# Thirteen embedding tables looked up by products instead of twelve, and gathers issued in step with TensorE's lookups

## The chip, the cores and the metric

The kernel runs on one core of a Trainium2 chip. The metric is the time of one execution on the device, in microseconds (us). The kernel before takes 147.07 us (median of 3 runs, 146.13 to 147.31).

## What is computed

A recommendation tower: 26 embedding tables are read at 512 samples, each sample's 27 vectors (the dense one and 26 rows) are multiplied with each other, and the 351 products above the diagonal go with the dense vector through three layers.

```python
e = jnp.stack([tbl_0[ids[:, 0]], ..., tbl_25[ids[:, 25]]], axis=1)        # 512 x 26 x 128, f32
combined = jnp.concatenate([dense[:, None, :], e], axis=1)                # 512 x 27 x 128
inter = jnp.einsum('bnd,bmd->bnm', combined, combined)[:, TRIU_I, TRIU_J] # 512 x 351
h = jnp.concatenate([dense, inter, dense], axis=1)                        # 512 x 607
h = jnp.maximum(h @ W_top1 + b_top1, 0.0)                                 # 512 x 512
h = jnp.maximum(h @ W_top2 + b_top2, 0.0)                                 # 512 x 256
y = h @ W_top3                                                            # 512 x 1
```

Tables have 1000, 1250, 12500 or (table 6) 125000 rows of 128 f32 values.

## The kernel before, in words

The 512 samples are four tiles of 128. A table's rows come to `xt` (128 features on the partitions; sample, table along the free dimension) in one of two ways.

**Lookup by product.** Twelve small tables (`ONEHOT_TABLES`) are loaded whole, with 8 rows to each of 125 partitions (10 rows for the one with 1250 rows; these counts are `CHUNKS`). For a lookup VectorE compares the ids of all 512 samples with the row numbers of each chunk (L552, one 125x512 mask for a chunk; the tables of a unit in `UNITS` are compared by one instruction, so a unit of two has masks of 125x1024). ScalarE makes the mask of the last chunk in two steps (L626, L631). ScalarE rounds the table to a high part (L616), VectorE subtracts that from the table, in two halves, for a low part (L561, `make_low`). TensorE then multiplies high and low part of each chunk with its mask (L363): 16 products for a table of 8 chunks, 20 for one of 10, all into one bank. ScalarE copies the bank to `xt` (L637). Two units of masks, two pairs of parts and four table buffers are in use in turn; a table's load waits until the low part of the table four before it is made. The last lookup is in two pieces, samples 0 to 127 before the first tile's products, the rest after them. A semaphore `lookup_done` counts the pieces.

**Gather.** The other 14 tables are gathered: GpSimd issues one indirect DMA (L332) for each table and tile, 128 rows of 512 bytes, 56 in all, tile by tile. After each one it writes a buffer that nobody reads (`unread`, L340) and waits for the write before that. From tile 2 on, a tile's gathers wait until the rows of the tile two before it have been taken. A tile's 14 tables are four groups (`GROUP_SIZES`); for a group TensorE transposes the rows (L377) and ScalarE copies them to `xt` (L644, one copy for each run of neighbouring tables). `AFTER_LOOKUP`, `IN_GRAM`, `IN_GAP`, `BEFORE_GRAM` and `AFTER_LAYER2` give the place of each of the 16 groups in TensorE's order.

**Products and layers.** For each sample there is one 27x27 product (L398, `gram`), in two halves of 64 samples for each tile; each is two matmuls in the trace, f32 operands being taken in two passes, so a half is 128 matmuls there. VectorE transposes the result into place and copies the triangle (L580, L591), TensorE turns it (L414), and the layers follow (L425, L436, L452). Products of tile t+1 stand between the halves of layer 1 of tile t. All orders are written out by hand; each engine runs its queue in order. W_top1 (1280 KB) is loaded by SyncE after the last table.

Of the kernel before, what the change touches and what calls it, by code (L numbers as in the profile page):

```python
# [29 lines left out]
F32 = mybir.dt.float32  # L30
# [5 lines left out]
P = 128  # L36
# [10 lines left out]

ONEHOT_TABLES = [4, 10, 11, 17, 19, 20, 24, 25, 3, 0, 8, 14]  # L50
VP = 125
CHUNKS = [8] * 9 + [10] + [8] * 2
CH = max(CHUNKS)
SIZES = sorted(set(CHUNKS))
FIRST_COLUMN = {c: sum(x + 1 for x in SIZES if x < c) for c in SIZES}
ROW_COLUMNS = sum(c + 1 for c in SIZES)

UNITS = [[0], [1, 2], [3, 4], [5, 6], [7, 8], [9], [10, 11]]
UNIT_OF = [u for u, members in enumerate(UNITS) for _ in members]
COMPARED = [CHUNKS[members[0]] - 1 for members in UNITS]  # L60
BEFORE_UNIT = [sum(COMPARED[:u]) for u in range(len(UNITS))]
UNIT_RING = 2
IDROW_RING = 3
SLOTS = max(CHUNKS[members[0]] * len(members) for members in UNITS)
assert sum(UNITS, []) == list(range(len(CHUNKS))) and all(len({CHUNKS[h] for h in m}) == 1 for m in UNITS)


LOW_BEFORE = []
_owed = []
for _u, _members in enumerate(UNITS):  # L70
    _end = COMPARED[_u]
# [6 lines left out]
VP_A = VP // 16 * 16  # L78
NOH = len(ONEHOT_TABLES)
TABLE_RING = 4  # L80
# [6 lines left out]

GATHERED = [f for f in range(F) if f not in ONEHOT_TABLES]
SOURCES = [f + 1 for f in GATHERED]
GROUP_SIZES = [4, 4, 3, 3]  # L90
GROUP_STARTS = [sum(GROUP_SIZES[:i]) for i in range(len(GROUP_SIZES))]
GROUPS = [(t, SOURCES[i:i + k]) for t in range(TILES) for i, k in zip(GROUP_STARTS, GROUP_SIZES)]
assert sum(GROUP_SIZES) == len(SOURCES)

AFTER_LOOKUP = [[], [], [], [0], [1], [2], [3], [4], [5], [6], [7], []]
IN_GRAM = [8]
IN_GAP = [9]
BEFORE_GRAM = [[], [], [14, 15]]  # L100
AFTER_LAYER2 = [[10, 11], [12, 13], []]
ORDER = sum(AFTER_LOOKUP, []) + IN_GRAM + IN_GAP
for _t in range(TILES - 1):
    ORDER += BEFORE_GRAM[_t] + AFTER_LAYER2[_t]
assert ORDER == list(range(len(GROUPS)))
GROUPS_UP_TO = [sum(t <= tile for t, _ in GROUPS) for tile in range(TILES)]

WARM_UP = 13
HIGH, LOW = PARTS = range(2)


# [43 lines left out]
def build(nc, dense_by_column, ids, ids_by_table, tables, w1, w2, columns, identity, out):  # L155
    with ExitStack() as ctx:
        def sb(name, shape, dt):
            return ctx.enter_context(nc.sbuf_tensor(name, shape, dt))

        def sem(name):  # L160
            return ctx.enter_context(nc.semaphore(name))
# [61 lines left out]
        lookup_done = sem("lookup_done")  # L223
# [3 lines left out]
        gram_done = sem("gram_done")  # L227
# [5 lines left out]
        h1_done = sem("h1_done")  # L233
# [8 lines left out]
        def unit_onehot(u, c):  # L242

            members = UNITS[u]
            chunks = CHUNKS[members[0]]
            slots = onehot[:, u % UNIT_RING, 0:len(members) * chunks, :]
# [25 lines left out]
        def load_first_table(queue, a, b):  # L272
            n = CHUNKS[0] * D
            rows = tables[ONEHOT_TABLES[0]].rearrange("(p c) d -> p (c d)", c=CHUNKS[0])
            queue.dma_start(table_sb[a:b, 0, 0:n], rows[a:b, :]).then_inc(table_landed[0], 16)

        unread = sb("unread", [P, 256], F32)
        unread_written = sem("unread_written")

        block = ctx.enter_context(nc.Block())  # L280

        @block.sync
        def _(sp):
            def load_table(h):
                s, f = h % TABLE_RING, ONEHOT_TABLES[h]
                u = UNIT_OF[h]
# [29 lines left out]
        @block.gpsimd  # L316
        def _(pool):

            for c in SIZES:
                first = FIRST_COLUMN[c]  # L320
                pool.iota(row_id[:, first:first + c], [[1, c]], base=0, channel_multiplier=c,
                          allow_small_or_imprecise_dtypes=True).then_inc(row_id_ready, 1)
                pool.iota(row_id[:, first + c:first + c + 1], [[1, 1]], base=1 - c, channel_multiplier=-c,
                          allow_small_or_imprecise_dtypes=True).then_inc(row_id_ready, 1)
            pool.wait_ge(ids_landed, 16)
            paced = 0
            for g, (t, features) in enumerate(GROUPS):
                if t >= ROWS_RING and t != GROUPS[g - 1][0]:
                    pool.wait_ge(group_turned, GROUPS_UP_TO[t - ROWS_RING])
                for n in features:  # L330
                    f = n - 1
                    pool.indirect_dma_start(  # L332
                        rows_sb[:, t % ROWS_RING, GATHERED.index(f), :], None, tables[f],
                        bass.IndirectOffsetOnAxis(ids_sb[:, t, f:f + 1], 0),
                    ).then_inc(group_landed[g], 16)

                    if paced:
                        pool.wait_ge(unread_written, paced)
                    paced += 1
                    pool.memset(unread[:, :], 0.0).then_inc(unread_written, 1)  # L340

        @block.tensor
        def _(pe):
# [141 lines left out]
            pe.wait_ge(zeros_ready, 1)  # L485
            for _ in range(WARM_UP):
                pe.matmul(ps_z[:, 0, :], zeros[:, 0:P], zeros[:, :], start=True, stop=True)  # L487


            for h in range(NOH):  # L490
                lookup(h)
                for g in AFTER_LOOKUP[h]:
                    turn_group(g)
            gram(0, 0)
            for g in IN_GRAM:
                turn_group(g)
            gram(0, 1)
            lookup(NOH - 1, 1)
            for g in IN_GAP:
                turn_group(g)  # L500
# [3 lines left out]
            for t in range(TILES - 1):  # L504

                layer1_pairs(t, 0)
                for g in BEFORE_GRAM[t]:
                    turn_group(g)
# [3 lines left out]
                for half in range(2):  # L512
                    layer2(t, half)
                for g in AFTER_LAYER2[t]:
                    turn_group(g)
# [91 lines left out]
        def _(act):  # L607
# [26 lines left out]
            def copy_lookup(h, piece=0):  # L634
                act.wait_ge(lookup_done, h + piece + 1)
                a, b = COLUMNS[h][piece]
                act.copy(xt[:, a // RUN:b // RUN, ONEHOT_TABLES[h] + 1, :],  # L637
                         ps_a[:, (h + piece) % 2, a:b].rearrange("p (q r) -> p q r", r=RUN)).then_inc(lookup_copied, 1)
# [61 lines left out]
            for h in range(NOH):  # L700
# [6 lines left out]
                if h == WORK_RING:  # L707
                    act.wait_ge(dense_landed, 16)
                    act.copy(xt[:, :, 0, :], dense_sb[:, :].rearrange("p (q r) -> p q r", r=RUN)).then_inc(dense_copied, 1)
                for g in AFTER_LOOKUP[h]:  # L710
                    copy_group(g)
            for g in IN_GRAM:
                copy_group(g)
            copy_lookup(NOH - 1, 1)
            for g in IN_GAP:
                copy_group(g)
            copy_z(0)
            for t in range(TILES - 1):
                relu1_low(t)
                for g in BEFORE_GRAM[t]:  # L720
                    copy_group(g)
                relu2(t)
                for g in AFTER_LAYER2[t]:
                    copy_group(g)
# [43 lines left out]
```

## Time and profile before

| what | us |
|---|---|
| median of 3 runs (146.13 to 147.31) | 147.07 |
| the profiled execution | 146.84 |
| its span, first to last instruction | 145.0 |
| PE, PEld busy | 112.2, 90.7 |
| DVE, ACT, POOL busy | 62.1, 50.5, 82.3 |

Mean granted clock of TensorE: 0.882 of full speed. The span is what the rows below count in; 1.8 us of the profiled execution's time lie outside it. PE is TensorE's matmuls, PEld its weight loads, DVE VectorE, ACT ScalarE, POOL GpSimd, SP SyncE. Matmuls overlap one another, so PE's busy time tells little in stretches of small products: there the distance from one start to the next is to be read.

### The profile page before, as it was taken

Reading aid. Unit: us, or ns where it says so; the run is one execution under the profiler, and the core shown is the slowest. Engines: PE = TensorE matmul, PEld = TensorE weight load, DVE = VectorE, ACT = ScalarE, POOL = GpSimd, SP = SyncE. Lnnn points to the kernel's source line nnn. Section 1 sums busy time; section 2 is a strip of 40 time slices with the busy share of each in tenths; the row PEclk is TensorE's granted clock in tenths of the full one; section 3 lists DMA queues with packets and bytes.
Section 4 is the critical chain, followed back from the end, with each engine's and each line's share of the span. In section 5 each row is a group of like instructions: output and inputs, shape, how many; then the busy total and the mean of one; then the engine's idle time right before and its main releaser. Section 6 shows DMA issues by size and latency. Waiting matters only on the chain.

```text
span 145.0 us, 3567 instructions
## 1 busy us (share of the span) xinstructions
PE 112.2 (77%) x1525; PEld 90.7 (63%) x1525; DVE 62.1 (43%) x124; ACT 50.5 (35%) x104; POOL 82.3 (57%) x120
## 2 busy tenths in 40 slices
PE   6988899999994699744223533289999999899993
PEld 2464578888882688622211311289999899689791
DVE  2999999999999945000000000041015015005010
ACT  4659829497775624100000000104104203500432
POOL 1999998999999899898989898900000000000000
PEclk9999999999999999975555555559999999999999
DMA  4899999598789221111211111100000000000000
GB/s 136 281 253 268 269 244 277 124 262 197 226 276 347 80 58 37 42 49 46 49 49 42 52 38 52 38 23 0 5 5 5 0 5 5 0 5 5 5 0 1
DMA packets 5535, 13.96 MB, mean 96 GB/s; under 512 B 1712, under 2 KB 2100, under 8 KB 5392
## 3 DMA queue, kind: packets, MB, share of 16 engines
q1 hardware_dynamic: 3558, 9.88, 23.9%
q0 software_dynamic: 1792, 3.67, 10.2%
q8 instruction: 12, 0.20, 0.6%
q10 hardware_dynamic: 170, 0.18, 0.5%
q14 instruction: 3, 0.02, 0.1%
HBM read 13.73 MB, written 0.00 MB: 95 GB/s over the span
## 4 chain that ended last, share of the span: by engine, by line
PE 45%; POOL 24%; issue 19%; DMA 6%; ACT 5%; ACTq 0%
POOL rows_sb L332 18%; PE ps_gram L398 17%; PE ps_a L363 9%; PE ps_a L436 9%; POOL unread L340 7%; PE ps_h L452 4%; DMA rows_sb<-tbl,ids_sb 4%; PE ps_rows L377 2%; ACT xt L644 2%; DMA ids_sb<-ids 2%; ACT table_sb L682 1%; PE ps_h L466 1%; PE ps_a L425 1%; PE ps_h L479 1%; PE ps_rows L466 1%
## 5 line engine op out<-in xcount | busy, mean ns | idle before, releaser
L332 POOL DMA_INDIRECT rows_sb<-tbl,ids_sb x56 | 60.6, 1083 | 11.4 <-issue 8.9
L363 PE MATMUL ps_a<-onehot,part_sb 125*128 125x512 f32 (+2 forms) x212 | 50.8, 390 | 2.1 <-DVE part_sb L561 1.3
L363 PEld LDWEIGHTS ps_a<-onehot,part_sb 125*128 125x128 f32 x212 | 38.1, 192 | 11.3 <-DVE part_sb L561 3.2
L398 PE MATMUL ps_gram<-xt 128*27 128x27 f32 x1024 | 25.3, 230 | 23.5 <-issue 22.7
L398 PEld LDWEIGHTS ps_gram<-xt 128*27 128x27 f32 x1024 | 20.1, 148 | 27.8 <-issue 25.9
L552 DVE TENSOR_SCALAR onehot<-idrow,row_id 125x1024 fp32r<-125x1024 int16 (+1 forms) x51 | 36.1, 763 | 1.7 <-DMA idrow<-ids_by_table 1.6
L580 DVE STREAM_TRANSPOSE table_sb<-ps_gram 128x864 f32<-128x864 f32 x3 | 3.2, 1083 | 42.2 <-PE ps_gram L398 42.2
L340 POOL MEMSET unread<- 128x256 f32 x56 | 21.2, 379 | 0.0
L644 ACT COPY xt<-ps_rows 128x256 f32<-128x256 f32 (+2 forms) x32 | 9.2, 359 | 30.8 <-remote 30.8
L561 DVE TENSOR_TENSOR part_sb<-table_sb,part_sb 125x512 fp32r<-125x512 f32 (+1 forms) x24 | 16.0, 689 | 2.7 <-issue 2.7
L637 ACT COPY xt<-ps_a 128x512 f32<-128x512 f32 (+2 forms) x13 | 7.2, 556 | 25.4 <-PE ps_a L363 24.3
L602 DVE TENSOR_SCALAR table_sb<-ps_a,columns_sb 128x128 f32<-128x128 f32 x8 | 2.4, 346 | 29.3 <-PE ps_a L436 29.3
L616 ACT CAST part_sb<-table_sb 125x1024 fp32r<-125x1024 f32 (+2 forms) x13 | 13.0, 1004 | 2.9 <-DMA table_sb<-tbl 2.9
L436 PE MATMUL ps_a<-table_sb,w_sb 128*128 128x128 f32 x96 | 13.0, 283 | 0.3
L436 PEld LDWEIGHTS ps_a<-table_sb,w_sb 128*128 128x128 f32 x96 | 11.4, 191 | 1.4 <-ACT table_sb L663 1.1
L377 PE MATMUL ps_rows<-ident_sb,rows_sb 128*128 128x128 f32 x56 | 8.8, 284 | 3.1 <-DMA rows_sb<-tbl,ids_sb 3.1
L377 PEld LDWEIGHTS ps_rows<-ident_sb,rows_sb 128*128 128x128 f32 x56 | 7.0, 146 | 5.8 <-issue 4.8
L682 ACT ACTIVATE table_sb<-ps_h,columns_sb 128x128 f32<-128x128 f32 x7 | 2.2, 364 | 23.0 <-PE ps_h L452 21.3
L626 ACT ACTIVATE distance<-idrow,row_id 125x1024 f32<-125x1024 int16 (+1 forms) x7 | 7.2, 1030 | 0.3 <-DMA idrow<-ids_by_table 0.3
L631 ACT ACTIVATE onehot<-distance 125x1024 fp32r<-125x1024 f32 (+1 forms) x7 | 6.6, 939 | 0.5
L452 PE MATMUL ps_h<-table_sb,w_sb 128*128 128x128 f32 x48 | 6.2, 281 | 0.0
L487 PE MATMUL ps_z<-zeros 128*128 128x512 bf16 x13 | 5.1, 577 | 1.2 <-DVE zeros L536 1.2
(36 smaller groups left out, 42.5 us busy)
## 6 DMA issues: line engine op xcount, KB each, us to landing
table_sb<-tbl SPq DMA_DIRECT2D x11, 448.0 KB
idrow<-ids_by_table SPq DMA_DIRECT2D x5, 256.0 KB
w_sb<-w SPq DMA_DIRECT2D x1, 1280.0 KB, 8.4
rows_sb<-tbl,ids_sb POOLq DMA_INDIRECT x56
table_sb<-tbl SPq DMA_DIRECT2D x1, 560.0 KB
table_sb<-tbl SPq DMA_DIRECT2D x10, 52.0 KB
w_sb<-w SPq DMA_DIRECT2D x1, 512.0 KB
dense_sb<-dense_by_column SPq DMA_DIRECT2D x1, 256.0 KB
```

Source lines behind the costliest of these rows:

```text
L332: pool.indirect_dma_start(rows_sb[:, t % ROWS_RING, GATHERED.index(f), :], None, tables[f], bass.IndirectOffsetOnAxis(ids_sb[:, t, f:f + 1 ...
L340: pool.memset(unread[:, :], 0.0).then_inc(unread_written, 1)
L363: last = pe.matmul(ps_a[:, (h + piece) % 2, a:b], parts_sb[part][:, w, c * D:(c + 1) * D], unit_onehot(u, c)[:, member, a:b], start=(part ...
L377: last = pe.transpose(ps_rows[:, g % 2, slot * P:(slot + 1) * P], rows_sb[:, t % ROWS_RING, GATHERED.index(n - 1), :], ident)
L398: last = pe.matmul(ps_gram[j * NPAD:j * NPAD + N, half, s * N:(s + 1) * N], x, x, start=True, stop=True)
L436: last = pe.matmul(ps_a[:, k, (m % 2) * P:(m % 2 + 1) * P], w1_sb[:, c, m * P:(m + 1) * P], zt[:, t % 2, c, :], start=False, stop=(c == ZC ...
L452: last = pe.matmul(ps_h2[:, 0, m * P:(m + 1) * P], w2_sb[:, k, m * P:(m + 1) * P], h1[:, t % 2, k, :], start=(k == 0 and m == 0), stop=(k ...
L552: dve.tensor_scalar(unit_onehot(u, c), idrow[0:VP, w, 0:n, :], row_id[0:VP, first + c:first + c + 1], None, ALU.is_equal).then_inc(onehot_ ...
L561: dve.tensor_tensor(parts_sb[LOW][:, w, columns], table_sb[0:VP, s, columns], parts_sb[HIGH][:, w, columns].bitcast(F32), ALU.subtract).th ...
L616: act.copy(parts_sb[HIGH][:, w, first:end], table_sb[0:VP, s, first:end]).then_inc(part_ready[HIGH], 1)
L626: act.activation(distance[:, 0:n, :], idrow[0:VP, w, 0:n, :], ACT.Abs, bias=row_id[0:VP, negated:negated + 1]) \
L644: last = act.copy(xt[:, t * P // RUN:(t + 1) * P // RUN, n:n + count, :].rearrange("p q n r -> p n q r"), ps_rows[:, g % 2, slot * P:(slot ...
```

## The change

A thirteenth lookup: tables 0 and 1, both of 1250 rows in 10 chunks, are fourth and seventh of the thirteen, each a unit of its own; before there was one table of 10 chunks (table 0), tenth of the twelve. There are 13 gathered tables instead of 14 and so 52 gathers, in groups of 4, 4, 3 and 2. The groups' places in TensorE's order follow. The unread buffer and its writes are gone. Gathers are now held back by semaphores: six are issued at once, then three for each piece that `lookup_done` counts up to thirteen; three of the last seven wait for the first tile's products (`gram_done`), four for its layer 1 (`h1_done` at 2).

```diff
-ONEHOT_TABLES = [4, 10, 11, 17, 19, 20, 24, 25, 3, 0, 8, 14]
+ONEHOT_TABLES = [4, 10, 11, 0, 17, 19, 1, 20, 24, 25, 3, 8, 14]
-CHUNKS = [8] * 9 + [10] + [8] * 2
+CHUNKS = [8] * 3 + ([10] + [8] * 2) * 2 + [8] * 4
-UNITS = [[0], [1, 2], [3, 4], [5, 6], [7, 8], [9], [10, 11]]
+UNITS = [[0], [1, 2], [3], [4, 5], [6], [7, 8], [9, 10], [11, 12]]
-GROUP_SIZES = [4, 4, 3, 3]
+GROUP_SIZES = [4, 4, 3, 2]
-AFTER_LOOKUP = [[], [], [], [0], [1], [2], [3], [4], [5], [6], [7], []]
-IN_GRAM = [8]
-IN_GAP = [9]
-BEFORE_GRAM = [[], [], [14, 15]]
-AFTER_LAYER2 = [[10, 11], [12, 13], []]
+AFTER_LOOKUP = [[], [], [], [0], [1], [2, 3], [4], [5], [6], [7], [8], [9], []]
+IN_GRAM = [10]
+IN_GAP = [11]
+BEFORE_GRAM = [[], [], [15]]
+AFTER_LAYER2 = [[12], [13, 14], []]
+GATHERS_PER_LOOKUP = 3
+GATHERS_AHEAD = 6
-        unread = sb("unread", [P, 256], F32)
-        unread_written = sem("unread_written")
...
-            paced = 0
+            issued = 0
             for g, (t, features) in enumerate(GROUPS):
                 if t >= ROWS_RING and t != GROUPS[g - 1][0]:
                     pool.wait_ge(group_turned, GROUPS_UP_TO[t - ROWS_RING])
                 for n in features:
                     f = n - 1
+                    if issued >= GATHERS_AHEAD and (issued - GATHERS_AHEAD) % GATHERS_PER_LOOKUP == 0:
+                        step = (issued - GATHERS_AHEAD) // GATHERS_PER_LOOKUP
+                        if step < NOH:
+                            pool.wait_ge(lookup_done, step + 1)
+                        elif step == NOH:
+                            pool.wait_ge(gram_done, 1)
+                        elif step == NOH + 1:
+                            pool.wait_ge(h1_done, 2)
+                    issued += 1
                     pool.indirect_dma_start(
                         rows_sb[:, t % ROWS_RING, GATHERED.index(f), :], None, tables[f],
                         bass.IndirectOffsetOnAxis(ids_sb[:, t, f:f + 1], 0),
                     ).then_inc(group_landed[g], 16)
-                    if paced:
-                        pool.wait_ge(unread_written, paced)
-                    paced += 1
-                    pool.memset(unread[:, :], 0.0).then_inc(unread_written, 1)
```

TensorE from the last lookups to the first tile's layer 1, in program order; the kernel before (`x64` counts a half's products, and an L363 row of 128 or 384 columns is a piece of the last lookup):

```order
L377 MATMUL ps_rows<-ident_sb,rows_sb 128x128 x3
L363 MATMUL ps_a<-onehot,part_sb 128x128 x16
L398 MATMUL ps_gram<-xt 27x27 x64
L377 MATMUL ps_rows<-ident_sb,rows_sb 128x128 x4
L398 MATMUL ps_gram<-xt 27x27 x64
L363 MATMUL ps_a<-onehot,part_sb 128x384 x16
L377 MATMUL ps_rows<-ident_sb,rows_sb 128x128 x4
L414 MATMUL ps_z<-ident_sb,table_sb 128x128 x3
L425 MATMUL ps_a<-dense_sb,w1d 128x128 x4
L436 MATMUL ps_a<-table_sb,w_sb 128x128 x6
L398 MATMUL ps_gram<-xt 27x27 x64
```

The same place in the changed kernel:

```order
L380 MATMUL ps_rows<-ident_sb,rows_sb 128x128 x4
L366 MATMUL ps_a<-onehot,part_sb 128x128 x16
L401 MATMUL ps_gram<-xt 27x27 x64
L380 MATMUL ps_rows<-ident_sb,rows_sb 128x128 x3
L401 MATMUL ps_gram<-xt 27x27 x64
L366 MATMUL ps_a<-onehot,part_sb 128x384 x16
L380 MATMUL ps_rows<-ident_sb,rows_sb 128x128 x2
L417 MATMUL ps_z<-ident_sb,table_sb 128x128 x3
L428 MATMUL ps_a<-dense_sb,w1d 128x128 x4
L439 MATMUL ps_a<-table_sb,w_sb 128x128 x6
L401 MATMUL ps_gram<-xt 27x27 x64
```

The order of stages is the same; within it there are three transposes instead of four between the halves and two instead of four behind the last piece.

GpSimd's queue at its end, in the changed kernel (before, each gather was followed by a memset of `unread`, and no gather waited for TensorE but the first of tiles 2 and 3):

```order
L340 DMA rows_sb<-tbl,ids_sb 128x128 [waits lookup_done,group_turned]
L340 DMA rows_sb<-tbl,ids_sb 128x128 x2
L340 DMA rows_sb<-tbl,ids_sb 128x128 [waits lookup_done]
L340 DMA rows_sb<-tbl,ids_sb 128x128 x2
L340 DMA rows_sb<-tbl,ids_sb 128x128 [waits gram_done]
L340 DMA rows_sb<-tbl,ids_sb 128x128 x2
L340 DMA rows_sb<-tbl,ids_sb 128x128 [waits h1_done]
L340 DMA rows_sb<-tbl,ids_sb 128x128 x3
```

The second wait for `lookup_done` there is for the thirteenth count, the last piece ahead of the first tile's products; so three gathers are issued from then on, three more after those products, and four after the first tile's layer 1.

## Rows read from the trace of the kernel before

**Rows 1.** The page: PE, POOL and TensorE's granted clock in 40 slices of the span, in tenths.

```profile
PE   6988899999994699744223533289999999899993
POOL 1999998999999899898989898900000000000000
PEclk9999999999999999975555555559999999999999
```

**Rows 2.** The page: the chain that ended last, share of the span by engine.

```profile
PE 45%; POOL 24%; issue 19%; DMA 6%; ACT 5%; ACTq 0%
```

**Rows 3.** Timeline of PE, first tile's products: start, duration, line, operands, count [idle before, releaser].

```profile
59.90 1.02 PE L398 MATMUL ps_gram<-xt 128*27 128x27 f32 x44 [0.40 <-issue]
61.35 0.33 PE L398 MATMUL ps_gram<-xt 128*27 128x27 f32 x5 [0.43 <-issue]
...
71.76 0.31 PE L398 MATMUL ps_gram<-xt 128*27 128x27 f32 x4 [1.13 <-issue]
...
80.53 1.11 PE L377 MATMUL ps_rows<-ident_sb,rows_sb 128*128 128x128 f32 x4
...
93.41 0.32 PE L398 MATMUL ps_gram<-xt 128*27 128x27 f32 x4 [0.50 <-issue]
94.82 1.45 PE L398 MATMUL ps_gram<-xt 128*27 128x27 f32 x86 [1.09 <-issue]
96.20 3.73 PE L363 MATMUL ps_a<-onehot,part_sb 125*128 125x384 f32 x16
```

**Rows 4.** Timeline of POOL: gathers (L332) and unread writes (L340), beside lookups and after them.

```profile
31.37 1.20 POOL L332 DMA_INDIRECT rows_sb<-tbl,ids_sb  x1 [0.17 <-issue]
...
33.06 1.44 POOL L332 DMA_INDIRECT rows_sb<-tbl,ids_sb  x1 [0.17 <-issue]
...
59.93 0.95 POOL L332 DMA_INDIRECT rows_sb<-tbl,ids_sb  x1 [0.17 <-issue]
...
93.09 0.95 POOL L332 DMA_INDIRECT rows_sb<-tbl,ids_sb  x1 [0.16 <-issue]
94.04 0.33 POOL L340 MEMSET unread<- 128x256 f32 x1
```

**Rows 5.** Busy time in stretches: stretch and length, engines busy (instructions), PEclk, DMA share, GB/s.

```profile
60.00:70.00 10.00, 4.46 (x94) 3.10 (x94) 0.00 (x0) 0.00 (x0) 8.86 (x14) 0.68 0.18 48
...
90.00:100.00 10.00, 6.39 (x119) 5.95 (x119) 2.11 (x10) 0.68 (x3) 3.87 (x7) 0.62 0.10 28
```

**Rows 6.** Timeline of PE in the lookups (L363) and their transposes (L377).

```profile
24.75 0.60 PE L377 MATMUL ps_rows<-ident_sb,rows_sb 128*128 128x128 f32 x4
25.11 3.88 PE L363 MATMUL ps_a<-onehot,part_sb 125*128 125x512 f32 x16
...
48.26 0.63 PE L377 MATMUL ps_rows<-ident_sb,rows_sb 128*128 128x128 f32 x4 [3.11 <-DMA rows_sb<-tbl,ids_sb]
48.64 4.80 PE L363 MATMUL ps_a<-onehot,part_sb 125*128 125x512 f32 x20
```

**Rows 7.** The chain in order of time, the one long piece that is a transfer.

```profile
42.44 5.68 DMA rows_sb<-tbl,ids_sb
```

**Rows 8.** Timeline of SP's queue: the issue of W_top1.

```profile
38.85 0.45 SPq L309 DMA_DIRECT2D w_sb<-w  x1
```

**Rows 9.** Timeline of DVE: compares of a pair and of a single table (L552), low part (L561).

```profile
14.90 2.27 DVE L552 TENSOR_SCALAR onehot<-idrow,row_id 125x1024 fp32r<-125x1024 int16 x3
...
40.88 2.77 DVE L552 TENSOR_SCALAR onehot<-idrow,row_id 125x512 fp32r<-125x512 int16 x5
43.57 1.54 DVE L561 TENSOR_TENSOR part_sb<-table_sb,part_sb 125x640 fp32r<-125x640 f32 x2
```

**Rows 10.** Timeline of PE, the second tile's products, second half, and what follows.

```profile
106.60 2.21 PE L398 MATMUL ps_gram<-xt 128*27 128x27 f32 x128
108.74 2.05 PE L452 MATMUL ps_h<-table_sb,w_sb 128*128 128x128 f32 x16
```

**Rows 11.** Timeline of ACT, rows copied before the last tile's products.

```profile
126.23 0.92 ACT L644 COPY xt<-ps_rows 128x256 f32<-128x256 f32 x3
```

## The prediction

> **What bounds the kernel now.** I read the slices first. POOL is busy until slice 26 and PE is busy nearly always, except from slice 17 to 25, where it falls to 2 to 5 tenths and its granted clock to 0.5 [rows 1]. The chain that ended last gives a quarter of the span to POOL and a fifth to "issue", time in which an engine waited for nothing that the profile shows [rows 2]. So one stretch is out of order, and the timeline of PE says which: the first tile's products. Their first 44 matmuls come in 1.02 us, then some 5 come every 0.75 us, later about 4 at a time with up to 1.1 us between, until 94.82, where 86 come in 1.45 us and the stage ends [rows 3]. The stage takes from 59.5 (the idle 0.40 ahead of the first row included) to 96.2 = 36.7 us; the second tile's second half of 128 matmuls takes 2.1 us [rows 10], so two halves and a turn of rows should take 4.4.
>
> What holds it? Nothing in TensorE's queue waits there. POOL is busy through that whole stretch with gathers, the last from 93.09 to 94.04, and 0.8 us behind its end TensorE runs free again, with the clock low for most of 90 to 100 [rows 3 to 5]. All later products, with no gather beside them, are fast. I take it that gathers (or the unread writes between them) keep TensorE from issuing short matmuls. Lookups are not hurt: 16 matmuls of 512 columns beside gathers take 3.88 us, tail of the last included, and 20 take 4.80, so 0.23 us each [rows 6].
>
> **The change, part by part**, on the profiled execution (span 145.0, time 146.8; that is 0.2 below the median of the runs).
>
> *The thirteenth lookup: +4.6.* It has 10 chunks, 20 matmuls; 20 at 0.23 [rows 6], and all of it lies on TensorE, the bound.
>
> *Transposes: +0.7 ahead, -0.7 behind.* 34 instead of 28 stand among the lookups: 6 more at 0.11 [the step between the starts in rows 6, 0.36 to 0.45 for four]. 13 instead of 20 are left behind the first tile. Part of those is hidden by ScalarE's copies, but before the last tile's products, three copies (0.92) become one of 256 columns [rows 11]. I take 0.7 back.
>
> *The wait for rows: -3.1.* Before, a group needed rows whose gather had been issued at 42.4, behind W_top1 (issued at 38.85), and landed 5.7 us later [rows 6 to 8]. Now six gathers lead and three follow per lookup: the seventh group's last row (the 24th gather) is issued after lookup 6 and needed after lookup 9, the tenth group's (34th) after lookup 10 and needed after 12. Two to three lookups of 4 us cover 5.7 us and the gather's own time. What was on the path is gone; it would come back if POOL fell behind.
>
> *VectorE: +1.8.* Single units cost it more. A table of 10 chunks alone is 9 compares at 0.54 and two halves of a low part at 0.77 = 6.4 us, where TensorE needs 4.6 and a turn. A pair of 8 chunks is 7 compares at 0.73 and four low halves at 0.62 (0.77 for 640 columns, here 512), 7.6 us for two lookups that with their turns take 8.1 [rows 6, 9]. So at the fourth lookup, where VectorE has no lead yet, TensorE waits about 1.5, at the seventh a lead has been built and some 0.3 is left. Bounds: 0 (the unread writes that VectorE's compares met are gone) and 3.6 (both deficits in full).
>
> The last piece ahead of the products thus ends at 59.5 + 4.6 + 0.7 - 3.1 + 1.8 = 63.5.
>
> *Gathers beside lookups.* One takes 1.20 to 1.44 there, 0.95 where VectorE rests [rows 4]. With 0.1 to 0.17 between them three take 3.9 to 4.8 us, about one lookup with its turn. POOL is near its own bound. From the end of the first slice, 3.6, where POOL gets busy [rows 1], at 1.42 each to 58.5, where I put VectorE's last part, and then 1.05, 45 gathers end at about 66.1; counted from the thirteenth `lookup_done` at 63.5, three end at 66.7. I take 67.3, a small lag included; 66.5 and 70.5 are the ends.
>
> *First tile's products: 36.7 becomes 7.9.* The first 44 matmuls run, then TensorE crawls (84 from 60.9 to 80.5, 4.3 per us) until 0.7 behind the last gather: 68.0. Of 128 some 70 are left, 1.1 us, then a turn 0.3 and the other half 2.0: 71.4.
>
> *To the second tile's second half: 10.4 before* (96.2 to 106.6), two transposes fewer: 10.2, so 81.6. Three gathers lie beside the last lookup's piece, which long matmuls cover.
>
> *The last four gathers: +4.0.* They start with `h1_done` 2, which is exactly where the second tile's second half begins. Four at 1.05 end at 85.9, TensorE is free at 86.6, and of 128 matmuls some 66 are left: 87.7 instead of 83.7. Bounds 0 and 5.
>
> *The rest:* 108.74 to 145.0 = 36.3, less 0.7: 35.6. Sum 87.7 + 35.6 = 123.3, and 1.8 outside the span: **125.1**.
>
> The clock: it fell within 60 to 70 (0.68), after PE had crawled, and rose within 90 to 100, after it ran free [rows 5]. A short relapse costs little in the products (86 in 1.45 us at half clock) but doubles what follows, a turn of four 1.11 against 0.6 [rows 3, 6]: 0 to 1.5 us in each of the two places, in the range only.
>
> On two points the profile and the Trainium skill are at odds. The rows show TensorE free of its crawl 0.8 us after the last gather. "SBUF — State Buffer", section "SBUF: two separate sides", says that DMA ports and engine ports are disjoint, so that neither slows the other; by that rule the gathers' transfers would not be the cause and this gain would not come.
>
> **Rivals.**
>
> *The crawl is not the gathers' (slower than before).* If it belongs to the first products themselves, moving gathers away changes nothing: the stage keeps its 36.7 us, and the lookup, VectorE's waits and transposes are added: 146.8 + 4.6 + 1.8 + 0.7 - 3.1 - 0.7 = 150.1. It decides if under 3 us of the 36.7 go. Against it stands the release right behind the last gather, at an unchanged clock. 4 in 100.
>
> *The unread writes were the cause, or kept apart gathers that alone do no harm.* Then neither stall is left: 63.5 + 0.4 + 4.3 = 68.2, + 10.2 + 2.1 + 35.6 = 116.1, time 117.9. The bursts come at all phases of a gather's cycle, which speaks for neither. 9 in 100.
>
> *Gathers without writes between them starve the lookups too.* If each lets through only the 4 to 5 matmuls that it did in the products' later part, three let through 13 of the 16 to 20 that a lookup needs, and the rest follow: about 0.9 us for each of 12 lookups, +10: 135. Against it: beside gathers lookups went at full rate, 7 to 8 matmuls to a gather. 8 in 100.
>
> *POOL cannot keep three per lookup.* With gathers at 1.6 (1.44 and a gap), 34 are done by 58.5 and 11 more at 1.05 end at 70.1; a lag of 3 also makes a group of rows late by 1 or 2: 129 to 130. The rows span 1.20 to 1.44, so its upper end would have to be the rule. 8 in 100. The same page, "A bandwidth-pool intuition that's wrong", gives a gather-like DMA of 620 ns about 3100 beside VectorE's two-port copies, five times; at five times 0.95 us the gathers alone would take over 200 us. The trace, at 1.5 times at most, does not agree.
>
> **Numbers.** The forecast has 71 in 100. Its own range is 120.5 to 129: 0 or 5 for the last four, 0 to 3.6 for VectorE, the clock, the lag. The range that holds 8 in 10 takes in most of the case without stalls and of the one with slow gathers: 118 to 131. A change of 1% is what these runs can tell. Slower 0.03, same 0.01, faster 0.96.
>
> **What would show it.** Right: TensorE's lookups run to about 63.5 with no wait for rows; a wait on `part_sb` or `onehot` of 1 to 2 us near the fourth lookup; products of the first tile in 6 to 9 us with a burst, a crawl until the last of three gathers, and a free run; the second tile's second half at 5 to 6 us beside four gathers. Wrong: idle time inside lookups put down to issue (starved), first products at 4.4 us (no stall), or still above 30; rows waited for in the lookups (POOL late).

## The result: 130.2 us against 146.9, and a kernel before that takes 117 us on other chips

The changed kernel takes 130.24 us (median of 4 runs, 129.83 to 131.57) against 146.89 for the kernel before; the ratio is 0.889, with a 95% interval of 0.881 to 0.897. The sum of the forecast gave 125.1, its range was 118 to 131. That is the smaller half of the story. The experiments below ran on three chips: on chip 8 the kernel before takes 147 us, on chips 1 and 13 it takes 117. On chip 13 the change is worth 1.6%. Which chip these first runs had is not on record; their times and traces are like those of chip 8. Times are medians of all runs; a ratio leaves out runs over some 1.5% above the fastest of their kernel.

### The profile after

The page of the changed kernel, 40 slices of a span of 128.0 us, as in [rows 1]:

```profile
PE   6998999799999999997242999972999999799992
POOL 1788798788887587875575052055000000000000
PEclk9999999999999999999955599997579999999999
```

The long trough of the kernel before is gone. Two short ones are left, slices 19 to 21 and 26 to 27 (the first slice is 0), each with POOL busy, and in each the granted clock falls to about 0.5.

TensorE's timeline there, columns as in [rows 3]:

```profile
57.80 0.60 PE L380 MATMUL ps_rows<-ident_sb,rows_sb 128*128 128x128 f32 x4
58.15 1.98 PE L366 MATMUL ps_a<-onehot,part_sb 125*128 125x128 f32 x16
62.72 0.86 PE L401 MATMUL ps_gram<-xt 128*27 128x27 f32 x47 [2.58 <-ACT xt L647]
63.98 0.34 PE L401 MATMUL ps_gram<-xt 128*27 128x27 f32 x6 [0.40 <-issue]
...
69.04 0.31 PE L401 MATMUL ps_gram<-xt 128*27 128x27 f32 x4 [1.12 <-issue]
...
70.45 0.96 PE L401 MATMUL ps_gram<-xt 128*27 128x27 f32 x50 [0.50 <-issue]
...
74.10 3.05 PE L366 MATMUL ps_a<-onehot,part_sb 125*128 125x384 f32 x16
...
83.64 1.21 PE L401 MATMUL ps_gram<-xt 128*27 128x27 f32 x51
85.26 0.32 PE L401 MATMUL ps_gram<-xt 128*27 128x27 f32 x6 [0.41 <-issue]
...
89.60 0.97 PE L401 MATMUL ps_gram<-xt 128*27 128x27 f32 x51 [1.10 <-issue]
90.50 3.78 PE L455 MATMUL ps_h<-table_sb,w_sb 128*128 128x128 f32 x16
```

Both product stages look as forecast, a burst of some 50, a crawl, a free run. But the first starts 2.6 us late, lasts to 74.1, and the layer 2 behind the second runs at the low clock, 3.78 us against 2.05 in [rows 10]. POOL (columns as in [rows 4]) shows why the first lasts so long:

```profile
57.35 1.02 POOL L340 DMA_INDIRECT rows_sb<-tbl,ids_sb  x1 [0.30 <-issue]
58.68 0.94 POOL L340 DMA_INDIRECT rows_sb<-tbl,ids_sb  x1 [0.30 <-issue]
61.99 0.94 POOL L340 DMA_INDIRECT rows_sb<-tbl,ids_sb  x1 [2.37 <-PE ps_a L366]
...
68.22 0.94 POOL L340 DMA_INDIRECT rows_sb<-tbl,ids_sb  x1 [0.30 <-issue]
```

and ScalarE, which copies the twelfth lookup:

```profile
61.24 0.59 ACT L640 COPY xt<-ps_a 128x512 f32<-128x512 f32 x1 [5.26 <-PE ps_a L366]
```

The twelfth lookup's matmuls were issued before 57.8, yet ScalarE and POOL, which both wait for its `lookup_done`, go on only at 61.2 and 61.99. So the three gathers meant for the last lookup and the three meant for the products all start behind that lookup's end (60.13), and six lie there instead of three. The late completion is not the only reason: e13 below has POOL behind as well, with no completion late. TensorE is free 1.3 us behind the last gather's end (68.22 + 0.94 = 69.16, free at 70.45).

A completion seen late was in the trace of the kernel before already, and the prediction did not read it. The rows that TensorE turned in the middle of its crawl, at 80.53 [rows 3], are copied by ScalarE only 9 us behind the turn's end:

```profile
90.58 0.65 ACT L644 COPY xt<-ps_rows 128x256 f32<-128x256 f32 x2 [30.78 <-remote]
```

### The profile page after: what moved, and what is told of

Its sections match the earlier page's. It is cut to its first block, busy times and chain, and to the rows that moved or that the text cites. A ratio compares the mean times of both kernels' runs of the same rounds, so it can differ in the third digit from the quotient of the medians.

```text
span 128.0 us, 3569 instructions
## 1 busy us (share of the span) xinstructions
PE 111.4 (87%) x1541; PEld 92.2 (72%) x1541; DVE 62.7 (49%) x135; ACT 53.2 (42%) x112; POOL 56.3 (44%) x60
## 4 chain that ended last, share of the span: by engine, by line
PE 68%; DVE 11%; issue 8%; DMA 6%; ACT 5%; SPq 1%
PE ps_a L366 28%; PE ps_gram L401 15%; PE ps_a L439 10%; DVE onehot L555 8%; PE ps_h L455 6%; PE ps_rows L380 4%; DMA table_sb<-tbl 4%; DVE part_sb L564 3%; PE ps_a L428 2%; DMA idrow<-ids_by_table 2%; ACT xt L647 1%; ACT part_sb L619 1%; PE ps_h L469 1%; ACT table_sb L666 1%; ACT table_sb L685 1%
## 5 line engine op out<-in xcount | busy, mean ns | idle before, releaser
L340 POOL DMA_INDIRECT rows_sb<-tbl,ids_sb x52 | 55.7, 1072 | 31.7 <-issue 14.3
L366 PE MATMUL ps_a<-onehot,part_sb 125*128 125x512 f32 (+2 forms) x232 | 53.9, 385 | 1.3 <-DVE part_sb L564 0.8
L366 PEld LDWEIGHTS ps_a<-onehot,part_sb 125*128 125x128 f32 x232 | 41.1, 188 | 10.5 <-ACT part_sb L619 1.2
L401 PE MATMUL ps_gram<-xt 128*27 128x27 f32 x1024 | 19.8, 230 | 11.2 <-issue 7.9
L401 PEld LDWEIGHTS ps_gram<-xt 128*27 128x27 f32 x1024 | 17.1, 149 | 14.3 <-issue 9.9
L564 DVE TENSOR_TENSOR part_sb<-table_sb,part_sb 125x512 fp32r<-125x512 f32 (+1 forms) x26 | 17.7, 704 | 2.6 <-issue 2.1
L619 ACT CAST part_sb<-table_sb 125x1024 fp32r<-125x1024 f32 (+2 forms) x14 | 14.2, 1024 | 4.8 <-DMA table_sb<-tbl 4.8
L647 ACT COPY xt<-ps_rows 128x128 f32<-128x128 f32 (+2 forms) x36 | 9.1, 324 | 9.7 <-PE ps_rows L380 9.7
L455 PE MATMUL ps_h<-table_sb,w_sb 128*128 128x128 f32 x48 | 7.9, 331 | 0.0
L455 PEld LDWEIGHTS ps_h<-table_sb,w_sb 128*128 128x128 f32 x48 | 7.2, 238 | 0.2
## 6 DMA issues: line engine op xcount, KB each, us to landing
idrow<-ids_by_table SPq DMA_DIRECT2D x2, 128.0 KB
```

Source lines behind the costliest of these rows:

```text
L340: pool.indirect_dma_start(rows_sb[:, t % ROWS_RING, GATHERED.index(f), :], None, tables[f], bass.IndirectOffsetOnAxis(ids_sb[:, t, f:f + 1 ...
L366: last = pe.matmul(ps_a[:, (h + piece) % 2, a:b], parts_sb[part][:, w, c * D:(c + 1) * D], unit_onehot(u, c)[:, member, a:b], start=(part ...
L401: last = pe.matmul(ps_gram[j * NPAD:j * NPAD + N, half, s * N:(s + 1) * N], x, x, start=True, stop=True)
L455: last = pe.matmul(ps_h2[:, 0, m * P:(m + 1) * P], w2_sb[:, k, m * P:(m + 1) * P], h1[:, t % 2, k, :], start=(k == 0 and m == 0), stop=(k ...
L564: dve.tensor_tensor(parts_sb[LOW][:, w, columns], table_sb[0:VP, s, columns], parts_sb[HIGH][:, w, columns].bitcast(F32), ALU.subtract).th ...
L619: act.copy(parts_sb[HIGH][:, w, first:end], table_sb[0:VP, s, first:end]).then_inc(part_ready[HIGH], 1)
```

## The experiments

All kernels but e7, e8 and e10 are edits of the changed one. e1 to e4 ran on chip 1, e5 to e10 on chip 8, e12 and e13 on chip 13. Each figure for the kernel before is from the same job.

### e1: no gather is held back (chip 1)

```diff
-                    if issued >= GATHERS_AHEAD and (issued - GATHERS_AHEAD) % GATHERS_PER_LOOKUP == 0:
...
-                            pool.wait_ge(h1_done, 2)
```

> The changed kernel with no semaphore holding back a gather (only the wait for free row buffers is left). Theory (gathers in flight hold TensorE's completions and short matmuls): POOL issues 52 gathers every 1.3 us from 3.4 to about 72, TensorE crawls in the first products until about 73, but the second tile's second half is free at 2.0 us and the clock stays up behind it: 123 to 126 us, against 130.2 for the changed kernel. Rival (the pauses that the waits make are what lets TensorE's lookups through): lookups without any pause starve, idle time inside them, 135 or more.

Measured: 116.8 us against 116.83 before (ratio 1.004, 0.993 to 1.014). Neither the theory nor the rival had foreseen the 116.83. All 52 gathers run on beside lookups and products, to slice 26 of 40, and TensorE does not crawl; it makes one pause of 0.8 us:

```profile
60.74 2.17 PE L393 MATMUL ps_gram<-xt 128*27 128x27 f32 x128 [0.40 <-issue]
62.84 0.55 PE L372 MATMUL ps_rows<-ident_sb,rows_sb 128*128 128x128 f32 x3
63.32 1.17 PE L393 MATMUL ps_gram<-xt 128*27 128x27 f32 x66
65.29 1.07 PE L393 MATMUL ps_gram<-xt 128*27 128x27 f32 x62 [0.79 <-issue]
```

That pause stands at the same place, behind 66 matmuls of the second half, in every trace of chips 1 and 13. It is 0.4 us in e4, where no gather lies there, and 0.5 to 1.1 in e1, e2, e3 and e13, where gathers do. So gathers are not enough to cause the crawl; something of the chip (or of the time) belongs to it.

### e2: the unread writes back, the new waits out (chip 1)

```diff
-                    if issued >= GATHERS_AHEAD and (issued - GATHERS_AHEAD) % GATHERS_PER_LOOKUP == 0:
...
+                    if issued > 1:
+                        pool.wait_ge(unread_written, issued - 1)
+                    pool.memset(unread[:, :], 0.0).then_inc(unread_written, 1)
```

> The changed kernel with the unread write behind each gather put back beside the new waits. Theory: the write only stretches the gather's cycle from 1.25-1.33 to 1.44-1.7 us; the 39 gathers meant for the lookups run late into the first products, so the crawl there lasts until about 72 to 76: 131 to 136 us. Rival (the write's gap protects TensorE): completions come on time, the crawl is shorter, and the time falls below 129.

The kernel that ran is not quite the one described there: it has the writes but none of the new waits, as the diff says. It is therefore the thirteenth table alone, with the pacing of before. Measured: 121.4 us against 116.83 (ratio 1.041, 1.028 to 1.053), slower by 4.6 us, which is what 20 matmuls at 0.23 us cost; four gathers fewer bring nothing that could be seen here. The expectation's numbers were for the crawl and say nothing here. Against e1 it differs by the writes alone, and they cost 4.6 us as well. VectorE's groups by form, e2 first, then e1 (count, busy us, mean ns):

```profile
L553 DVE TENSOR_SCALAR onehot<-idrow,row_id 125x1024 fp32r<-125x1024 int16 x35 | 28.4, 869 | 0.9 <-PE ps_a L364 0.9
L553 DVE TENSOR_SCALAR onehot<-idrow,row_id 125x512 fp32r<-125x512 int16 x25 | 13.2, 585 | 1.6 <-DMA idrow<-ids_by_table 1.6
```

```profile
L547 DVE TENSOR_SCALAR onehot<-idrow,row_id 125x1024 fp32r<-125x1024 int16 x35 | 24.4, 755 | 0.5 <-PE ps_a L358 0.4
L547 DVE TENSOR_SCALAR onehot<-idrow,row_id 125x512 fp32r<-125x512 int16 x25 | 10.6, 479 | 1.2 <-DMA idrow<-ids_by_table 1.2
```

A compare of the same shape takes 0.11 us less without them, 6.6 us of VectorE's time in all. TensorE's longest wait for a low part falls from 2.0 to 0.8 us, and two waits for rows, 1.0 together, go; but two waits for a high part, 1.3 together, come. These waits do not add up to 4.6. Behind the 2.0 wait e2's granted clock is 0.66 from 30 to 35 us, which takes a part; the rest was not traced to a line.

### e3: the last four gathers behind the second tile's products (chip 1)

```diff
                         elif step == NOH + 1:
-                            pool.wait_ge(h1_done, 2)
+                            pool.wait_ge(gram_done, 2)
```

> The changed kernel with the last four gathers waiting for the second tile's products instead of the first tile's layer 1. Theory: the second tile's second half falls from 6.9 to 2.0 us and layer 2 from 3.8 to 2.0 (the clock stays up), all the rest as it was: 123 to 125 us. Rival (gathers hold layer 2, turns and their completions as much as products): the stall only moves behind, 128 to 131 us.

Measured: 115.38 us against 116.83 (ratio 0.992, 0.982 to 1.001): without the crawl nothing stands there to be gained. Layer 2 beside two of the four takes 2.40 us at the full clock, against 2.05 with no gather beside it in [rows 10], so of the stall that the rival expected there only 0.35 us is seen.

### e4 and e6: no gather meant to lie beside products (chips 1 and 8)

```diff
+HELD = {6 + 3 * k: ("lookup", k + 1) for k in range(11)}
+HELD.update({39: ("gram", 1), 45: ("gram", 2), 50: ("gram", 3)})
...
+                    if issued in HELD:
+                        which, count = HELD[issued]
+                        pool.wait_ge({"lookup": lookup_done, "gram": gram_done}[which], count)
```

> The changed kernel with no gather meant to lie beside any products: 39 gathers in step with eleven lookups, then 6 behind the first tile's products, 5 behind the second's, 2 behind the third's. Theory: first products in 4.5 to 6 us instead of 14, the second tile's as in the run before: 113 to 117 us. Rival (the lost time is a delay of TensorE's completions that does not depend on gathers beside products): 122 or more.

> The kernel of e4 (no gather meant to lie beside any products) once more, for a second chip or time. Where the kernel before takes about 147: 113 to 118 us by the theory that gathers beside products are the whole cause, 122 or more if completions are delayed without them. Where the kernel before takes about 117: 115 to 116, as in e4.

Measured: e4 115.63 us against 116.83 (0.993, 0.983 to 1.002); e6, on the chip with the crawl, 122.79 against 147.37 (0.838, 0.832 to 0.844), 9.9 below the changed kernel in the same job (e5). TensorE's timeline of e6:

```profile
63.00 1.99 PE L398 MATMUL ps_gram<-xt 128*27 128x27 f32 x128 [1.72 <-issue]
64.92 0.90 PE L377 MATMUL ps_rows<-ident_sb,rows_sb 128*128 128x128 f32 x3
65.75 2.15 PE L398 MATMUL ps_gram<-xt 128*27 128x27 f32 x128
...
73.96 0.69 PE L398 MATMUL ps_gram<-xt 128*27 128x27 f32 x27
75.78 0.32 PE L398 MATMUL ps_gram<-xt 128*27 128x27 f32 x5 [1.13 <-issue]
77.24 1.58 PE L398 MATMUL ps_gram<-xt 128*27 128x27 f32 x96 [1.14 <-issue]
```

Where no gather lies beside products they take 2 us a half on this chip too. Six gathers behind the first tile last until 75.87, into the second tile's first half, and it crawls until 77.24. With the same work in the same job as e5, this shows that the crawl comes with gathers beside products. But the theory that they are the whole cause is missed: the 122.79 us lie where the rival had them (122 or more, completions late without gathers beside products), and the trace has both. The first products start at 63.0 instead of 60.2 in e4, with 1.0 us of idle time inside the lookups put down to issue; the rest above e4 is mostly the crawl in the second tile and another one in the third.

### e5, e9 and e13: the changed kernel again (chips 8, 8 and 13)

> The changed kernel once more, unaltered, beside the kernel before. In the runs that the prediction was scored by the kernel before took 146.9 us and crawled in its first products for 34 us; in the job of e1 to e4 the same kernel took 116.8 and did not crawl. Theory (the crawl beside gathers is a condition of a chip or of a time, and the change gains only under it): where the kernel before takes about 117, the changed one takes 114.5 to 118 (ratio 0.98 to 1.01), with products at 2.0 us a half beside gathers; where it takes about 147, the changed one takes 130. Rival (the changed kernel itself makes TensorE wait, whatever the chip): it takes 125 or more in either case.

> The changed kernel a third time, for the pair of kernels on a chip without the crawl. Without it: 115 to 117.5 us, ratio 0.98 to 1.01, as e1 and e3 gave with the same thirteen tables and other waits; with it 130 to 133. Rival: 120 or more without the crawl, if its waits cost what they bring.

> The changed kernel a fourth time, for the pair of kernels on a chip without the crawl. Without it: 115 to 117.5 us, ratio 0.98 to 1.01, as e1 and e3 gave with the same thirteen tables and other waits; with it 130 to 133. Rival: 120 or more without the crawl, if its waits cost what they bring.

Measured: e5 132.65 us against 147.37 (0.898, 0.892 to 0.904), above the 130 that it was expected to take; e9 130.91 against 146.87 (0.892, 0.887 to 0.897); e13, on a chip without the crawl, 115.09 against 117.44 (0.984, 0.975 to 0.993). The pair's gain is thus 15 to 16 us with the crawl and about 2 without, by the interval 0.8 to 2.9.

In e5 and e9 the stage from the end of the last lookup's first piece to the end of the first products takes 13.8 and 14.0 us, as in the first trace (14.0), and six gathers start in it each time. But which completion is late differs. In e5 it is the eleventh lookup's, done at 54.8, and TensorE starts its products amid a row of gathers (POOL goes on from 58.8 to 69.7):

```profile
58.54 0.59 ACT L640 COPY xt<-ps_a 128x512 f32<-128x512 f32 x1 [3.35 <-remote]
64.91 0.72 PE L401 MATMUL ps_gram<-xt 128*27 128x27 f32 x34 [2.50 <-issue]
```

In e9 it is the last piece's, done at 61.2:

```profile
66.89 0.27 ACT L640 COPY xt<-ps_a 128x128 f32<-128x128 f32 x1 [5.01 <-remote]
67.25 0.85 PE L401 MATMUL ps_gram<-xt 128*27 128x27 f32 x46 [6.04 <-issue]
```

TensorE, POOL and ScalarE in e13, at the same place in the program as above:

```profile
58.33 0.60 PE L380 MATMUL ps_rows<-ident_sb,rows_sb 128*128 128x128 f32 x4
58.68 1.98 PE L366 MATMUL ps_a<-onehot,part_sb 125*128 125x128 f32 x16
61.07 2.18 PE L401 MATMUL ps_gram<-xt 128*27 128x27 f32 x128 [0.40 <-issue]
63.18 0.55 PE L380 MATMUL ps_rows<-ident_sb,rows_sb 128*128 128x128 f32 x3
63.66 1.18 PE L401 MATMUL ps_gram<-xt 128*27 128x27 f32 x66
65.93 1.08 PE L401 MATMUL ps_gram<-xt 128*27 128x27 f32 x62 [1.10 <-issue]
...
76.47 2.09 PE L401 MATMUL ps_gram<-xt 128*27 128x27 f32 x128
78.50 2.45 PE L455 MATMUL ps_h<-table_sb,w_sb 128*128 128x128 f32 x16
```

```profile
60.92 0.95 POOL L340 DMA_INDIRECT rows_sb<-tbl,ids_sb  x1 [0.30 <-issue]
62.18 0.94 POOL L340 DMA_INDIRECT rows_sb<-tbl,ids_sb  x1 [0.30 <-issue]
...
65.92 0.94 POOL L340 DMA_INDIRECT rows_sb<-tbl,ids_sb  x1 [0.30 <-issue]
...
76.82 0.94 POOL L340 DMA_INDIRECT rows_sb<-tbl,ids_sb  x1 [6.09 <-PE ps_a L439]
```

```profile
58.52 0.59 ACT L640 COPY xt<-ps_a 128x512 f32<-128x512 f32 x1 [2.00 <-PE ps_a L366]
```

Gathers lie beside the same products, each 0.94 to 0.95 us long with 0.30 between, as on chip 8. Two halves take 2.1 to 2.2 us; the one with the pause of 1.10 takes 3.3. So gathers may cost TensorE some tenths of a microsecond here too, but it does not crawl. The copy of the twelfth lookup starts 0.2 us behind the turn that follows that lookup; on the chip with the crawl it was 3.4 us behind it. So the gathers' own pace does not differ between the chips; what differs is how soon TensorE's work is seen as done and how it goes on beside them.

e13 also shows what POOL's queue is worth by itself. No completion is late, yet the last gather ahead of the wait for the first products ends at 66.86, 6.2 us behind the lookups' end (60.66), and not the 3.8 that the prediction had. The last piece is short: with its turn it takes 2.3 us, and the three gathers released by the twelfth lookup need 3.75.

### e7 and e10: twelve tables, no unread writes (chip 8)

e7 has the waits of the change (six ahead, three for each piece, nine behind the first tile's products, five behind its layer 1); e10 has them placed as in e6:

```diff
+HELD = {6 + 3 * k: ("lookup", k + 1) for k in range(11)}
+HELD.update({39: ("gram", 1), 46: ("gram", 2), 53: ("gram", 3)})
-                    if paced:
-                        pool.wait_ge(unread_written, paced)
-                    paced += 1
-                    pool.memset(unread[:, :], 0.0).then_inc(unread_written, 1)
```

> The kernel before with its twelve tables, but the unread writes taken out and gathers held by lookup_done (six ahead, three for each piece), nine behind the first tile's products and five behind its layer 1: the pacing without the thirteenth table. Theory: under the crawl it gains nearly all that the changed kernel gains, 126 to 133 us against 147; without the crawl it saves the 3 us wait for rows at most, 111 to 115 us against 117, and is 3 to 4 us faster than the changed kernel, since it has one lookup of 4.6 us less. Rival (the thirteenth table is what pays, by four gathers fewer): it is no faster than the changed kernel without the crawl.

> Twelve tables, no unread writes, no gather meant to lie beside products: 39 gathers in step with lookups, then 7, 7 and 3 behind the products of tiles 1, 2 and 3. Theory (without the crawl the thirteenth lookup costs 4.6 us and buys nothing): 111 to 114 us without the crawl, the fastest so far; with it 119 to 126. Rival (VectorE or the table loads set the pace of the lookups, and gathers fewer are worth having): 115 or more without the crawl.

Measured: e7 137.05 us against 147.37 (0.932, 0.927 to 0.937), outside its range of 126 to 133; e10 128.04 against 146.87 (0.872, 0.867 to 0.876), 2.0 above its range for the crawl. Their chip crawls, so what twelve tables take without it was not seen. TensorE and POOL in e7:

```profile
54.51 1.98 PE L364 MATMUL ps_a<-onehot,part_sb 125*128 125x128 f32 x16
62.54 0.74 PE L399 MATMUL ps_gram<-xt 128*27 128x27 f32 x37 [6.05 <-issue]
```

```profile
60.18 0.94 POOL L338 DMA_INDIRECT rows_sb<-tbl,ids_sb  x1 [0.30 <-issue]
62.41 0.94 POOL L338 DMA_INDIRECT rows_sb<-tbl,ids_sb  x1 [1.29 <-remote]
```

The lookups end at 56.5, TensorE stands for 6.05 us, and goes on 1.4 behind the end of the last of a row of gathers without a pause (61.12). POOL is the bound here: it issues the gathers meant for the lookups until 61 whether there are twelve lookups or thirteen (in e6 until 61.5), and in this trace TensorE starts its products behind them (in e5 it did not wait for the row's end). With the same placement, thirteen tables take 122.8 (e6) and twelve 128.0 (e10), so the thirteenth table pays where the crawl is. The likely reason, argued and not tested alone, is that its 4.6 us lie in time that TensorE would stand idle, and that four gathers less remain.

### e8: the kernel before, traced again (chip 8)

> The kernel before, unaltered, for a trace of it on this job's chip. Where it takes about 117 us the theory expects: first products in 4.4 us with gathers beside them, lookup_done seen within 0.2 us of each lookup's last matmul, no idle time put down to issue but short pieces. Where it takes about 147, the crawl of 34 us as in the trace before. Rival (the chips differ in how fast they gather): gathers or their transfers are slower where the kernel crawls.

Measured: 147.04 us, ratio to the kernel before 1.001 (0.998 to 1.005). On this chip, it crawls as in [rows 3], from 60.9 on; no trace of it without the crawl was taken. The rival is refuted by e13 and e9, in which gathers take 0.94 us alike.

### e12: plain loads beside the first products (chip 13)

```diff
+            sp.wait_ge(lookup_done, NOH)
+            for k in range(12):
+                sp.dma_start(plain_sb[:, k, :], tables[2][k * P:(k + 1) * P, :]).then_inc(plain_landed, 16)
+            sp.wait_ge(plain_landed, 192)
```

> The kernel of e4 and e6 with 12 plain loads of 64 KB (128 rows of 512 bytes each, unread) issued by SyncE from the thirteenth lookup_done on, so that transfers of SyncE's queue lie beside the first products and no gather does. Without the crawl nothing changes, 115 to 117 us. With the crawl: if any transfer of small rows makes TensorE crawl, the first products take 7 us or more instead of 4.8; if only GpSimd's gathers do, they stay at 4.4 to 5 and the time at 122 to 124.

Measured: 116.03 us against 117.44 (0.987, 0.981 to 0.994), as expected where there is no crawl. The transfers do lie beside the first products (DMA share 0.36 there, 0.02 in e4); the pause behind 66 matmuls is 0.9 us against 0.4 in e4, one trace each. The question it was made for, whether plain transfers make TensorE crawl as gathers do, stays open. The same kernel with sixteen loads (e11) never ran: its buffer of 8192 bytes for each partition is larger than the 6432 left.

## Why the prediction was right, and where its sum was off

The time lies inside the range, at its upper end (one of the four runs, 131.57, lies above it), and the direction and the mechanism were right for the chip at hand: TensorE crawls through short matmuls while gathers run, and is free 0.8 to 2.0 us behind the last. That the forecast was made for a chip that crawls was luck; nothing in its one trace said that others do not. Point by point, against the span of 123.3 that the sum gave (128.0 measured):

- **Lookups to 63.5: they ended at 60.1 (-3.4).** The thirteenth lookup took its 4.6 and the wait for rows is gone, as forecast. The mis-sized term is VectorE's +1.8; with the other terms as forecast, it would have to be -1.6, beyond its lower bound of 0. The wait on `part_sb` was 0.8 us at the fifth lookup, where 1 to 2 near the fourth was to be seen, and VectorE gained by the removal of the unread writes: compares of 1024 columns fell from 840 to 756 ns, of 512 from 593 to 484. The prediction named this gain but gave it no size of its own; e1 against e2 shows it as a saving of 4.6 us where nothing else differs.
- **First products 7.9 us: they took 14.0 (60.1 to 74.1, +6.1).** This step failed in size. The last gather was to end 3.8 us behind the lookups and ended 9.0 behind them (69.16). 2.4 of the 5.2 us come from POOL's queue, which is behind even where no completion is late (6.2 in e13): the step counted three gathers from the thirteenth `lookup_done` and left out those of the twelfth that are still to be issued. The other 2.8 are of this chip, where the step took `lookup_done` as being seen when the lookup is done, and POOL stood for 2.37 us. The remaining 0.9 is TensorE's later release (1.3 instead of 0.7 us) and a slower turn at the low clock.
  The two errors hang together. POOL's row, not the lookups' end, says when the products are over, so most of what the lookups saved was lost again; the sum took them as added up. Against the clock, the products were over at 74.1 and not at 71.4, 2.7 us late.
- **To the second half 10.2: 9.5 (-0.7).**
- **The last four gathers, 6.1 for the half: 6.9 (+0.8).** Place, number and end were as forecast.
- **The rest 35.6: 37.5 (+1.9).** 1.7 of it is layer 2 at the low clock, which the text had left to the range at 0 to 1.5.

The working's check on POOL has a slip: 38.7 gathers at 1.42 and 6.3 at 1.05 end at 65.2, not 66.1. The sum did not use it. The case "POOL cannot keep three per lookup" gave 129 to 130; POOL was late indeed, by a few gathers at the end and not for want of speed throughout, and no group of rows was waited for in this trace (0.7 and 0.4 us in e5 and e9).

The rivals: that the unread writes were the cause is refuted, since the crawl is there without them (after, e5 to e7). Starved lookups were not seen in this trace, 16 matmuls in 3.9 us; in e5, e6, e7 and e10 idle time inside lookups put down to issue is 1.0 to 2.1 us in all, far from the 10 of the rival. Their completion was held too, a form that no rival had. "The crawl is not the gathers'" is refuted on chip 8 by e6, where products without gathers beside them are fast. The rule that ports of transfers and of engines are disjoint ("SBUF — State Buffer", section "SBUF: two separate sides", in the Trainium skill) is thus no guide to the time on chip 8; whether ports are what gathers and TensorE meet at there, no run shows. On chips 1 and 13 the traces are near the rule, 2.0 to 2.2 us a half with gathers beside it but for the one pause.

What makes the chips differ was not found: the gathers' durations (0.94 us) and cadence (1.25 us) are the same. Chip and time are not fully apart either, since chips 1 and 13 were used once each and chip 8 twice, in between. Two further candidates can be held against the traces. TensorE's supply of instructions: in the kernel before, one block of 16 KB came on the instruction queue in all 34 us of the crawl, at 69.1 to 70.6, so no such transfer was under way in its first 8 us. The recording of the run itself: every run on record carries a recorded span and clock, and in the traces with the crawl the recording has gaps. The packed trace of the changed kernel holds 985 semaphore updates where that of e13, the same program, holds 1977; e6 has 1001 where e4 has 1988. Whether the gaps and the crawl have one cause is not shown, nor whether TensorE crawls in a run that is not recorded.

The forecast thus rested on one trace from a chip with the crawl. The change's worth there, 15 to 17 us, is nearly all the removal of a stall that other chips do not have; without it, the sum of its parts is -4.6 (the writes, e1 against e2), +4.6 (the thirteenth lookup, e2 against before), and 1 to 2 us gained by the waits (e3 and e4, whose waits differ from the change's, take 1.4 and 1.2 less than e1 in one job; e13 and e1, each against its own kernel before, are at 0.984 and 1.004). The intervals of these ratios touch, so the last part is the least sure.

## What to carry to other kernels

A stage in which an engine idles with nothing to wait for, and whose end coincides with another engine's last instruction, is worth an experiment that moves that other work away, before anything is made faster: e6, with the same work as the changed kernel and only the gathers' places altered, gained 9.9 us more on the chip that crawls and lost nothing on chip 1 (e4 against e1 and e3). Work held back "in step" by a completion should be given slack of some lookups at its end: its engine can be behind by its own pace, as POOL in e13, and the completion can be seen late, as on chip 8. And before a gain is believed, the kernel before should be timed on more than one chip: here 147 and 117 us were both steady, and repeated runs agreed within 2% on chip 8 and within 3% on chips 1 and 13, but for one run of 315.6 us on chip 13.

## What the runs showed that I had not expected

- The same kernel takes 147 us on one chip and 117 on two others, over 7 or more runs each time. The traces of the changed kernel differ in how TensorE goes on beside gathers, in how soon its work is seen as done, and in how many semaphore updates were recorded.
- On the chip with the crawl, completions of TensorE's matmuls beside gathers can be seen 3 to 6 us late (after, e5, e7, e9) and in the kernel before 9, while others, beside gathers too, are seen at once. Some come behind the end of a row of gathers, some in the middle of one; what decides it was not found.
- Without the unread write, POOL's gathers are not 0.1 apart, as assumed, but 0.30: 1.25 us each where VectorE rests, against 1.44 with the write.
- The writes of 128x256 f32, read by nobody, cost VectorE 0.11 us for each compare (e2 against e1).
